# Four products of one column half, then four of the other: the order inside a gram half of a DLRM tower

## What is computed

```python
x = layer_norm(dense_t @ Wd.T, gd, bd)
y = layer_norm(jnp.einsum('bnd,ed->bne', sparse_t, Ws), gs, bs)
y = layer_norm(jnp.einsum('bne,pn->bep', y, Wsi), gsi, bsi)      # 32 projected features of 128
T = jnp.concatenate([x[:, None, :], jnp.swapaxes(y, 1, 2)], axis=1)
Z = jnp.einsum('bnd,bmd->bnm', T, T)                             # the gram matrix
out = layer_norm(Z[:, TRIL_I, TRIL_J] @ Wl.T, gl, bl)            # then mask, concat, a three-layer MLP
```

## Time and profile before

| | |
|---|---|
| median of the three runs | 182.55 us (181.4 to 182.62) |
| the profiled execution: span from its first to its last instruction | 216.2 us |
| TensorE matmuls busy in it | 163.0 us, 75% |
| VectorE, ScalarE, GpSimd busy | 120.7, 78.7, 107.9 us |
| mean granted TensorE clock | 0.865 of full speed |
| gram matmuls (L487) | 512 in 32 halves, 24.4 us busy |

### The profile page before, as it was taken

One profiled execution on the slowest core, in us unless ns is written; L12 is line 12 of the kernel. 1 busy time (PEld: TensorE's weight loads), 2 busy tenths in 40 slices (PEclk: granted clock), 3 DMA queues, 4 the chain that ended last, 5 costly groups with the idle time before them and its releaser, 6 DMA issues.

```text
span 216.2 us, 3315 instructions
## 1 busy us (share of the span) xinstructions
PE 163.0 (75%) x1189; PEld 110.3 (51%) x1189; DVE 120.7 (56%) x325; ACT 78.7 (36%) x221; POOL 107.9 (50%) x139
## 2 busy tenths in 40 slices
PE   0373406489859698686699689789969999978985
PEld 0171303354645356444275576385649676448574
DVE  1405200997384445766665818559548689876410
ACT  2103001051546354414424234444233655463152
POOL 4777774571665646667545666656755000352000
PEclk9996555859979799969589959799997999999999
DMA  6211891010111101231001112211101011000000
GB/s 210 82 28 26 270 352 25 12 27 15 18 24 20 27 16 21 52 78 37 18 17 23 26 27 55 70 30 24 25 18 28 19 49 33 0 2 3 0 0 0
DMA packets 9730, 9.76 MB, mean 45 GB/s; under 512 B 3666, under 2 KB 7378, under 8 KB 9459
## 3 DMA queue, kind: packets, MB, share of 16 engines
q0 software_dynamic: 3328, 3.41, 8.1%
q1 hardware_dynamic: 5954, 5.18, 7.6%
q10 hardware_dynamic: 432, 0.97, 1.4%
HBM read 7.98 MB, written 0.00 MB: 37 GB/s over the span
## 4 chain that ended last, share of the span: by engine, by line
PE 45%; another core or an unknown queue 17%; DVE 16%; ACT 10%; issue 9%; DMA 2%; SPq 0%; ACTq 0%; DVEq 0%
PE pz L487 7%; PE pc L451 6%; PE pf L503 5%; PE py L472 4%; PE tu L434 4%; PE pf L529 3%; PE tu L424 3%; PE pf L522 3%; DVE y_ms L1091 3%; ACT gram L783 2%; PE py L503 2%; PE py L467 2%; DMA proj_w<-proj_w_dram 2%; PE pf L605 2%
## 5 line engine op out<-in xcount | busy, mean ns | idle before, releaser
L389 POOL DMA_INDIRECT emb<-tables_dram,rows_at x104 | 100.0, 961 | 61.2 <-PE tu L424 26.4
L487 PE MATMUL pz<-T 128*64 128x67 f32 x512 | 24.4, 242 | 9.7 <-ACT gram L783 4.0
L451 PE MATMUL pc<-wbd,emb 128*128 128x192 f32 (+4 forms) x128 | 30.0, 344 | 1.4 <-issue 1.1
L451 PEld LDWEIGHTS pc<-wbd,emb 128*128 128x128 f32 x128 | 20.7, 206 | 20.1 <-issue 17.1
L487 PEld LDWEIGHTS pz<-T 128*64 128x64 f32 x512 | 19.9, 149 | 18.4 <-issue 12.9
L1091 DVE TENSOR_REDUCE y_ms<-ysq 128x16 f32<-128x512 f32 x32 | 20.4, 679 | 12.6 <-ACT ysq L772 12.4
L757 ACT ACTIVATE embT<-tu 128x256 f32<-128x256 f32 x26 | 9.9, 380 | 43.3 <-PE tu L424 31.0
L434 PE MATMUL tu<-mbd,embT 128*128 128x128 f32 x104 | 19.2, 313 | 3.8 <-issue 2.3
L472 PE MATMUL py<-cs,wg 64*128 64x512 f32 x64 | 21.1, 746 | 0.0
L783 ACT ACTIVATE gram<-pz 128x268 f32<-128x268 f32 x32 | 12.5, 389 | 23.7 <-remote 12.6
L1100 DVE TENSOR_TENSOR T<-py,y_r 128x512 f32<-128x512 f32 x32 | 20.6, 687 | 0.6
(11 more groups left out here) (142 smaller groups left out, 208.4 us busy)
## 6 DMA issues: line engine op xcount, KB each, us to landing
emb<-tables_dram,rows_at POOLq DMA_INDIRECT x104, 2.4
z<-gram SPq DMA_DIRECT2D x48, 32.0 KB
w<-w_dram SPq DMA_DIRECT2D x1, 1280.0 KB
wl<-wl_dram SPq DMA_DIRECT2D x1, 1024.0 KB
denseT<-denseT_dram ACTq DMA_DIRECT2D x1, 512.0 KB
w<-w_dram SPq DMA_DIRECT2D x1, 512.0 KB
comb_w<-comb_w_dram ACTq DMA_DIRECT2D x1, 311.0 KB, 3.3
sel<-sel_dram SPq DMA_DIRECT2D x1, 240.0 KB
```

The source lines that it names most:

```text
L389: pool.indirect_dma_start(emb[:, 2 * pair + half, :], None, t["tables"], bass.IndirectOffsetOnAxis(ap=rows_at[:, 2 * g + half, j:j + 1], a ...
L451: mm = pe.matmul(PC[m % NPC][:, :, :].rearrange("p b c -> p (b c)")[:, col:col + n], of, wbd[:, :, :].rearrange("p b c -> p (b c)")[:, at: ...
L487: mm = pe.matmul(PZ[2 * PR * h:2 * PR * h + 2 * PR, ITEMS * b:ITEMS * (b + 1)], of[:, 0:2 * PR], of, start=True, stop=True)
```

## The change

Inside a gram half the two loops are exchanged. Before, the calls go to the column halves in turn: (b0,h0), (b0,h1), (b1,h0), (b1,h1) and so on. Now they go (b0,h0), (b1,h0), (b2,h0), (b3,h0), (b0,h1), (b1,h1), (b2,h1), (b3,h1). The calls themselves, their operands and outputs are the same, the last call is the same one (b3,h1), and it still releases `z_done`. No wait, copy or DMA is added, removed or moved.

```diff
@@ -481,8 +481,8 @@
                 wait_if_any(pe, gram_ready, 2 * m + half)
                 at = QS // 2 * (2 * (m % BLOCKS) + half)
-                for b in range(SLOTS):
-                    for h in range(2):
+                for h in range(2):
+                    for b in range(SLOTS):
                         of = T[:, at + 2 * b + h, :]
                         mm = pe.matmul(PZ[2 * PR * h:2 * PR * h + 2 * PR, ITEMS * b:ITEMS * (b + 1)],
                                        of[:, 0:2 * PR], of, start=True, stop=True)
```

## The result

The changed kernel takes **188.11 us** (median of 4 runs, 187.86 to 188.24) beside 182.17 us for the kernel before in the same series (181.4 to 182.62): a ratio of 1.0391, 95% interval 1.0342 to 1.0441. It is slower by 5.9 us, where no change was forecast.

What follows compares the result with a forecast made beforehand. TensorE was taken to bound the kernel, with 45% of the chain of waits. 32 gram halves x 0.02 = 0.64 us, x 0.62 on the path, gave 0.4 us; 182.55 + 0.4 = 182.95 us, range 181.0 to 188.0.

Steps and rivals of the forecast that it cites:

- The share of time on the path: Gram line L487: some 0.62 of what a gram half gains or loses was taken to be on the path.
- That two column halves work at once: Gram half: both column halves work at the same time, 8 slots in place of 16, 0.45 us for 0.90.
- I therefore take it that the second half is served almost at once: Gram half after the change: the second column half's start is 0.012 us late, taken as 0.02.
- a full one stops only its own: Inside TensorE: each column half has its own line of waiting instructions, and a full line stops only that half.
- the term of the sum: Gram halves: 32 halves x 0.02 = 0.64 us of TensorE, x 0.62 on the path = 0.4 us.
- The 40 instructions: Gram half in the earlier trace: 40 instructions passed on and waiting in TensorE, against 16 instructions of one column half.
- at least 7 places: Rival 2's reading of 33 against 40 held instructions: a column half's line has at least 7 places.
- The second rival: Gram half: a line of middling length lets the second half in 4 slots late; 187.6 us, chance 0.10.
- The first rival: Gram half: column halves follow each other, second starting 7 slots later; 191.5 us, chance 0.16.
- The clock: Third rival, TensorE's clock from 43.7 to 145 us: a tenth less time at half clock; 181 us, chance 0.08.

Runs made afterwards that it cites:

- runs of two, three and four: Gram call orders A A B B A A B B, A A A B B B A B and A B B B B A A A, against the kernel before: 182.87, 186.45 and 187.49 us.
- A B A B A B A B: Order of the kernel before, A being column half h = 0 and B h = 1: 182.17 us in the changed kernel's series.
- A A B B A A B B: Gram calls two of column half h = 0 (A), two of h = 1 (B), and again, against the kernel before: 182.87 us, ratio 1.0047.
- A B B A A B A B: Gram calls in this order of column halves (A h = 0, B h = 1), against the kernel before: 181.4 us, ratio 1.0024.
- A A A B B B A B: Gram calls three of column half h = 0 (A), three of h = 1 (B), then one each, against the kernel before: 186.45 us, ratio 1.0213.
- A B B B B A A A: Gram calls one of column half h = 0 (A), four of h = 1 (B), three of A, against the kernel before: 187.49 us, timed once.
- the second profile of before: The kernel before, unchanged, profiled once more: 180.56 us; span 178.8 us at mean clock 0.971.
- The first profile: The kernel before as profiled for the prediction: span 216.2 us at mean clock 0.865.
- A A A A B B B B: Order of the change, all calls of column half h = 0 (A), then of h = 1 (B), against the kernel before: 188.11 us, ratio 1.0391.

## Why the prediction was wrong

- **The share of time on the path** was put at 0.62 from the chain. Measured: 5.9 of 9.0 us, 0.66, by the medians, and 0.84 by the spans of the two profiles at like clock (186.4 and 178.8); the second figure is rather too high, since 180.56 us lies below the median of its series. That step held, if low.
- **That two column halves work at once** in 8 slots for 16, and that a call of one half goes past waiting work of the other, held: every experiment shows it.
- **The step that failed** is "I therefore take it that the second half is served almost at once", with its premise that of the lines for the two halves "a full one stops only its own". The second half's delay was put at 0.012 to 0.02 us and is 0.29 us; the term of the sum was 0.64 us of TensorE and measured 9.0. A full line stops the program for the other half too: the wait at L122 came 0.31 us after the half's start and not 0.04. The 40 instructions that had been passed on the earlier trace rows were taken for places in which a column half's work can wait. Only about 6 places for each half let the other half go on. The rest of the 40, by the reading in the next point, stand in a common line ahead of the point where work is dealt out to the halves, and in that line nothing passes anything.
- **The trace of before held this number.** 40 were found with two column halves at work and 33 with the whole array as one. If the common line has 28 places and each half 6, the counts are 28 + 2 x 6 = 40 and 28 + 6 = 34. The prediction read the difference of 7 as a lower bound ("at least 7 places") and then reasoned with the 40. That the length of a half's line is about 6 is shown by runs of two, three and four; the 28 is a reading of the counts, and 34 is one more than the 33 found. The traces after bear it out. The wait at L122 stands behind 44 instructions, so with 28 places it can begin once 16 of them have been dealt out. With 6 waiting in each line that is almost at once for A B A B A B A B, A A B B A A B B and A B B A A B A B, with A's third matmul (0.17 us after the start) for A A A B B B A B, with B's third (0.18) for A B B B B A A A, and with A's fifth (0.29) for the change. In that half of each trace the wait began at 0.04 us in the first three, then at 0.20, 0.20 and 0.31: 0.02 to 0.04 us behind each. With 27 places it would have come later in the first, with 29 earlier in the last, by some 0.05 us.
- **The second rival was right**, in mechanism and nearly in size: it had the second half let in 4 slots late, for 8.2 us of TensorE and 187.6 us; the measured are 5 slots, 9.0 us and 188.11 us. It was given 0.10. That it comes so near is in part luck: it counted five halves at half clock, of which the trace after has none, and so made up for the slot that it lacked.
- **The first rival was wrong**: the Trainium skill's rule (TensorE: Matmul & The Clock Gate, Part 3, "What overlaps and what doesn't"), strict program order for matmuls, gave 191.5 us. The trace after disagrees with it as that of before did: the second half's first pass starts beside the first half's fifth, three passes early. The same page's section "The mechanism" states a "64-deep reorder window", for weight loads to row groups that do not conflict or to the background weight buffer. The trace after gives no such reach between the two column halves, which use the same rows: 15 instructions were too many.
- **The clock** decided nothing in the comparison: 0.963 after, 0.971 in the second profile of before; 0.943 to 0.973 in the timed runs after, 0.941 to 0.972 in those of before in the next series. The first profile's 0.865 made the gram look 2.3 us costlier than it is at full clock.

## What to carry to other kernels

Where small float32 matmuls share the array by column halves, write their calls so that the halves alternate. A run of calls of one half costs time when it fills that half's line and the other half runs out of work meanwhile: beside the 0.47 us of a gram half from first to last start, A A B B A A B B cost 0.05 us more, A A A B B B A B and A B B B B A A A 0.17, and A A A A B B B B 0.28, while A B B A A B A B cost nothing. Other shapes than this one were not tried. A count of instructions that an engine has taken in does not tell how many can be passed over; look at the difference between the counts in two situations before the total. And where a mechanism is known to reach some distance and the change needs five times that, the case in which it does not reach deserves more than the 0.26 that the first two rivals had here together.

## What the runs showed of the hardware

A column half of the array takes passes of 67 columns at one in 0.057 us whether the other half is at work or not, and both at once where the program feeds them. About 6 instructions (weight loads and matmuls, both counted) can wait in one half's line; the seventh holds back the program for both. That fits all six orders timed: 22.1 us busy for A B A B A B A B, 22.6 for A B B A A B A B, 23.7 for A A B B A A B B, 27.5 and 27.6 for A A A B B B A B and A B B B B A A A, 31.1 for the change.
